# Attention scores on 62 and 64 array rows instead of 48 and 50, the added rows filled by zeros

## The reference

```python
h = layernorm(x) * (1 + ca) + sa
q, k, v = split(h @ w_in.T)                  # 16 heads, Hd = 16, N = 1024
scores = einsum('bhqd,bhkd->bhqk', q, k) * Hd ** -0.5
scores = where(causal, -inf, scores)
x = x + ga * ((softmax(scores) @ v) @ w_out.T + b_out)
h = layernorm(x) * (1 + cb) + sb
x_prev = shift_by_one_token(h)
xr = mu_r * h + (1 - mu_r) * x_prev;  xk = mu_k * h + (1 - mu_k) * x_prev
x = x + gb * sigmoid(xr @ W_r.T) * (square(relu(xk @ W_k.T)) @ W_v.T)
```

## Time and profile before

| what | value |
|---|---|
| median of 3 runs | 2016.91 us (1999.79 to 2022.92) |
| the profiled execution | 2004.49 us |
| its span, first to last instruction | 2002.6 us |
| around the span | 1.9 us |
| TensorE busy | 1685.5 us, 84% |
| VectorE, ScalarE, GpSimd busy | 1106.7, 917.5, 614.1 us |
| mean granted TensorE clock | 0.784 |

### The profile page before, as it was taken

One profiled execution on the slowest core, in us unless ns is written; L12 is line 12 of the kernel. 1 busy time (PEld: TensorE's weight loads), 2 busy tenths in 40 slices (PEclk: granted clock), 3 DMA queues, 4 the chain that ended last, 5 costly groups with the idle time before them and its releaser, 6 DMA issues.

```text
span 2002.6 us, 34555 instructions
## 1 busy us (share of the span) xinstructions
PE 1685.5 (84%) x10856; PEld 939.6 (47%) x10856; DVE 1106.7 (55%) x2246; ACT 917.5 (46%) x1859; POOL 614.1 (31%) x750
## 2 busy tenths in 40 slices
PE   4798898888888888889888898988888888889855
PEld 2443444444544445445444445444454444544444
DVE  4666546656465554655557454565546566555332
ACT  2055445455345543455445443545534545444522
POOL 2012112323333231343224333232333323233454
PEclk7596858678886987778796787768778687977865
DMA  2311131111221122111211113111122112211010
GB/s 89 78 39 39 47 84 47 33 44 47 80 59 36 46 57 72 42 46 44 84 44 48 33 49 87 47 33 46 44 81 61 33 38 61 65 40 49 28 48 16
DMA packets 79864, 103.37 MB, mean 52 GB/s; under 512 B 22576, under 2 KB 43320, under 8 KB 79680
## 3 DMA queue, kind: packets, MB, share of 16 engines
q1 hardware_dynamic: 76544, 91.86, 17.0%
q0 software_dynamic: 2560, 8.39, 1.1%
q10 hardware_dynamic: 576, 0.79, 0.2%
HBM read 31.74 MB, written 8.94 MB: 20 GB/s over the span
## 4 chain that ended last, share of the span: by engine, by line
PE 64%; DVE 14%; ACT 9%; issue 8%; POOL 2%; DMA 1%; SPq 1%; ACTq 0%; DVEq 0%; POOLq 0%
PE val_ps L1120 16%; PE col_ps L1051 13%; PE dense_ps L1130 9%; PE row_ps L1088 8%; DVE max_a L874 7%; PE dense_ps L1131 6%; PE dense_ps L1132 6%; PE row_ps L1099 4%; PE dense_ps L1149 3%; ACT weights L715 3%; ACT h_hi L758 1%; PE row_ps L1069 1%; DVE mix_out L990 1%; DVE stats_c L900 1%; ACT k_part L746 1%
## 5 line engine op out<-in xcount | busy, mean ns | idle before, releaser
L715 ACT ACTIVATE weights<-col_ps 128x512 f32<-128x512 f32 (+2 forms) x1280 | 631.7, 558 | 675.6 <-PE col_ps L1051 674.5
L874 DVE TENSOR_REDUCE max_a<-row_ps 128x1 f32<-128x512 f32 (+3 forms) x896 | 541.9, 644 | 357.4 <-PE row_ps L1099 255.9
L1088 PE MATMUL row_ps<-k_stack,q_stack 48*128 48x512 f32 (+3 forms) x1536 | 462.9, 458 | 83.8 <-DVE max_a L874 64.4
L1051 PE MATMUL col_ps<-q_stack,k_stack 50*128 50x512 f32 (+3 forms) x1536 | 460.1, 492 | 87.0 <-ACT weights L715 79.7
L604 POOL TENSOR_SCALAR_AFFINE_SELECT weights<-weights 128x512 f32<-128x512 f32 x256 | 164.4, 642 | 877.0 <-ACT weights L715 875.2
L1120 PE MATMUL val_ps<-weights,v_ones 128*32 128x512 f32 (+3 forms) x3072 | 417.3, 623 | 4.7 <-POOL weights L604 4.5
L1051 PEld LDWEIGHTS col_ps<-q_stack,k_stack 50*128 50x128 f32 x1536 | 208.3, 219 | 329.3 <-ACT weights L715 194.5
L1088 PEld LDWEIGHTS row_ps<-k_stack,q_stack 48*128 48x128 f32 x1536 | 242.1, 236 | 196.1 <-DVE max_a L874 142.0
L874 DVE TENSOR_REDUCE max_b<-row_ps 128x1 f32<-128x384 f32 (+3 forms) x384 | 214.3, 594 | 205.1 <-PE row_ps L1099 203.1
L1099 PE MATMUL row_ps<-mask_fill,mask_ident 64*128 64x64 bf16 (+1 forms) x2048 | 172.2, 240 | 0.0
L1099 PEld LDWEIGHTS row_ps<-mask_fill,mask_ident 64*128 64x128 bf16 x2048 | 88.0, 113 | 42.0 <-issue 32.5
(11 more groups left out here) (122 smaller groups left out, 2191.6 us busy)
## 6 DMA issues: line engine op xcount, KB each, us to landing
q_stack<-q_part SPq DMA_DIRECT2D x384, 64.0 KB, 2.2
k_stack<-k_part SPq DMA_DIRECT2D x372, 64.0 KB, 2.2
xa<-in_x SPq DMA_DIRECT2D x8, 1024.0 KB, 5.6
att<-val_out SPq DMA_DIRECT2D x64, 128.0 KB
recips<-recip_rows SPq DMA_DIRECT2D x32, 256.0 KB
xq<-in_x SPq DMA_DIRECT2D x28, 256.0 KB, 4.0
out<-xq POOLq DMA_DIRECT2D x28, 256.0 KB, 2.7
q_stack<-max_rows SPq DMA_DIRECT2D x256, 4.0 KB
```

The costliest lines, as they stand in the source:

```text
L715: nc.scalar.activation(weights[:, t % 2, heads[0]:heads[-1] + 1:2, 0:q1 - q0], col_ps[bank][:, 0:n * (q1 - q0)].rearrange("p (h q) -> p h ...
L874: nc.vector.reduce_max(dest, bank[:, 0:len(heads) * (k1 - k0)].rearrange("p (h k) -> p h k", h=len(heads)), AX_X).then_inc(max_done, 1)
L1051: last = nc.tensor.matmul(col_ps[bank][:, i * (q1 - q0):(i + 1) * (q1 - q0)], stack_at(k_stack[s % 2], rows, heads[i], P * j, P * (j + 1)) ...
L1088: last = nc.tensor.matmul(banks[odd][:, n * width:(n + 1) * width], stack_at(q_stack[stack], rows, heads[n], P * i, P * (i + 1)), stack_at ...
```

## The change

The two rows with the maximum move from 48 and 49 of each half to 62 and 63 (`MAX_AT`), in `place_max`. Column scores read all 64 rows of a half, row scores 62 rows. Rows 48 to 61 of both `q_stack` buffers are set to zero once, by two memsets on POOL in the setup; in `k_stack` those rows are ones as before, so the products there are zero. The same matmuls run in the same order, and each writes what it did.

```diff
@@ -44,6 +44,7 @@
 MROWS = 2
 ROW_TILE = 64
+MAX_AT = ROW_TILE - MROWS
@@ -463,7 +464,7 @@ place_max
-                        row, lo = ROW_TILE * odd + ROWS + part, 8 * (2 * part + odd)
+                        row, lo = ROW_TILE * odd + MAX_AT + part, 8 * (2 * part + odd)
@@ -569,8 +570,10 @@ setup of POOL
-            nc.gpsimd.memset(neg_half[:], -0.5).then_inc(consts_zero, 1)
-            pool.wait_ge(consts_zero, 1)
+            nc.gpsimd.memset(neg_half[:], -0.5)
+            for stack in q_stack:
+                nc.gpsimd.memset(stack[:].bitcast(F32), 0.0).then_inc(consts_zero, 1)
+            pool.wait_ge(consts_zero, 2)
@@ -1047,7 +1050,7 @@ score_columns
-                        rows = slice(ROW_TILE * odd, ROW_TILE * odd + ROWS + MROWS)
+                        rows = slice(ROW_TILE * odd, ROW_TILE * (odd + 1))
@@ -1083,7 +1086,7 @@ row_pair
-                        rows = slice(ROW_TILE * odd, ROW_TILE * odd + ROWS)
+                        rows = slice(ROW_TILE * odd, ROW_TILE * odd + MAX_AT)
```

## The result

| | before | after |
|---|---|---|
| median of 4 runs, us | 2015.77 (1999.79 to 2022.92) | 1951.78 (1943.63 to 1962.56) |
| ratio, 95% interval | | 0.9696 (0.9618 to 0.9774) |
| the profiled execution, us | 2004.49 | 1943.63 |
| its span, us | 2002.6 | 1941.7 |
| mean granted TensorE clock | 0.784 | 0.830 |

The kernel is 3.0% faster; 8.7% was forecast (1840 of 2016 us). The time lies in the stated range (1755 to 1975), but the size is a third of what was said. Rival 1 gave 1941 us at a clock near 0.83, and that is what the profiled execution shows.

The account below looks back on a forecast made before the run. TensorE, busy 84% of the span at a mean clock of 0.784, was taken as the bound. 2002.6 (span) - 165 (clock) + 0 (rows) + 0 (setup) = 1838, plus 1.9 around it: 1840 us, range 1755 to 1975.

Parts of the forecast that it names:

- Rival 1: Whole kernel: only one fill counts, or the effect is proportional to added rows; clock near 0.83, 1941 us; chance 0.20.
- That only the clock could carry a gain: TensorE's granted clock: the one large term, 165 us off the span, with all other terms zero.
- Setup and widening at zero: POOL's two memsets, 3.5 us, hidden under 21 us idle; wider score operands add no matmul time: both zero.
- rival 2: TensorE's clock: no effect, it ignores rows or zeros don't count; 2004 us within 1%; chance 0.13.
- The price of 1.45: Whole span: 1.45 us at half clock hold the work of 1 us at full clock, taken from repeated steps and quarters.
- 1735 / (1 - 0.31x) + 2: Whole kernel: time in us with share x at half clock; 1735 us is the span wholly at full clock.
- The upper bound of 47 ns for two rows more: Score matmuls: if the step from 48 to 50 rows were real, widening would cost at most 72 us; zero was taken.
- I take it that the fill lifts quarters 1 and 3 to what quarter 2 shows now, 0.88, and quarters 0 and 2 to the best that a quarter 0 shows now, 0.94: Clock in the four quarters of a batch: mean rises to 0.91, span falls to 1838 us, 165 us less.
- VectorE's maxima are late next: TensorE's waits for VectorE's maxima: next limit if TensorE gets faster; VectorE already busy 81% of a full-clock pair of steps.
- Rival 3: Whole kernel: nearly always full clock, quarters at 0.97, 1770 us; chance 0.08.
- Rival 4: Step 4 of quarter 3 and its like in quarters 0 and 1: gaps lower the clock, 2047 us; chance 0.07.

Follow-up runs that it names:

- e5: Changed kernel with both scores on 32 rows of a half, a third of the score products and the column scores' maximum left out: 2147.18 us, 1.073 of before.
- e1: Changed kernel with row scores back on 48 rows, column scores staying on 64: 1970.19 us, 0.990 of the kernel before.
- e3: Changed kernel with column scores back on 50 rows and taken without the maximum, row scores staying on 62: 1971.31 us, 0.989 of the kernel before.
- e2: Changed kernel with row scores on 64 rows too, so both kinds read 64: 1949.96 us, 0.982 of the kernel before.
- e6: Changed kernel with VectorE's maxima taken over the first half of each block's keys: 1848.45 us, 0.926 of the kernel before.
- e4: Changed kernel with both kinds of scores on 48 rows, column scores taken without the maximum: 2005.55 us, 1.004 of the kernel before.
- e8: Changed kernel with a 256-column product of zeros ahead of column-score pairs except in steps 1 and 5: 1936.97 us, 0.972 of the kernel before.
- e15: Changed kernel with row scores on 64 rows and two 512-column products of zeros ahead of each column-score pair in steps 0, 3, 4, 11: 1924.36 us.

## Why the prediction was partly right

- **That only the clock could carry a gain: right.** The score matmuls' own time is the same at the same clock (437 and 483 ns), and untouched groups got faster.
- **Setup and widening at zero: right**, 3.55 us under an idle time that still has 17.71 us.
- **Busy time alone does not set the clock (against rival 2): right.** 98% busy at half clock was the pointer; e5 is the proof in the other direction, with TensorE 87% busy at a clock of 0.706, where the kernel before has 84% at 0.784 and the changed one 83% at 0.830. The reading of the Trainium skill ("TensorE: Matmul & The Clock Gate", Part 1: The HAM clock gate) as busy time alone would have left 2004 us, and these runs do not agree with it.
- **The price of 1.45: right.** The formula 1735 / (1 - 0.31x) + 2 gives, with each profile's own clock, 1941 us for the changed kernel (1943.63 measured), 1960 for e1 (1967.26), 1971 for e3 (1966.19), 1937 for e2 (1943.15). It does not hold where the work changes: e6 lies 79 us under it, and e5, far outside the clocks it was taken from, 43 us over.
- **The upper bound of 47 ns for two rows more: a misreading that cost nothing.** It set column scores on 50 rows against row scores on 48; e4's column scores on 48 rows take 483 ns. That ScalarE's banks explain the difference was not tested.
- **"I take it that the fill lifts quarters 1 and 3 to what quarter 2 shows now, 0.88, and quarters 0 and 2 to the best that a quarter 0 shows now, 0.94": wrong.** This is the failed step, a term whose mechanism is right and whose size is not. It took 0.91 for a clock that measured 0.830, so 165 us where 61 came. Four things it left out. It read the clock of quarter 2 as a level that any richer work reaches, though quarter 2 adds whole products of 128 rows, far more than 14 rows of zeros. It laid 0.91 over the whole span, also over the first 92.3 and the last 107.6 us, which hold almost no scores and stood at 0.66 each before the change: by its own formula about 31 us of the 165, an estimate from these windows. It treated the falls as rare accidents that a little help avoids, from the one pair of quarters 3 in which batch 4 and batch 5 differ; but 45 of 57 falls sit in the same two steps of every quarter, and 40 of 60 do with the fill. And it ignored that the waits in the timeline, cited beside a fall, are untouched by the change. How much each of the four weighs was not measured, and why the rise stopped at 0.83 stays open.
- **"VectorE's maxima are late next": of no weight for the clock.** The idle time before the row scores rose from 83.8 to 95.0 us, and 67.5 of it is VectorE's, 3.1 us more than before. Taking half of the keys out of the maxima gave time and hardly any clock (e6).
- **Rival 1: right in time (1941), clock (0.83) and, as far as shown, its second mechanism**, the effect in proportion to the added rows: either fill alone gives about half. Its first, that the row scores' fill to 62 counts for nothing, has e2 (1950 us, no further gain at 64) and e3's clock (0.803 to 0.824) against it. It had a chance of 0.20. That it hit the time to 3 us of the profiled execution is partly luck: its mean came from thirds chosen by hand. Quarter 1 did come to its 0.77, but quarter 2 did not rise, and a quarter of the gain came in batch 0, which no part of the prediction looked at.
- **Rival 3: not seen.** No quarter has a mean of 0.97.
- **Rival 4: not seen.** Quarter 3 has a mean of 0.83 over batches 1 to 6, against 0.78 before, and no run with the fill was slower.

## What to carry to other kernels

Where TensorE is busy all the time and its granted clock still swings, look at what the matmuls occupy as well as at the gaps: here paired matmuls on a part of each half's rows could be padded with zero rows at no cost of their own (437 and 483 ns for 435 and 482), and 14 rows more in 28% of the matmuls gave 2 to 3%. Before forecasting how far a clock will rise, list the places where it falls, over all batches and not in one: this change left those places as they were and only shortened the stretches behind them. And lay a forecast clock only over the stretches that hold the changed work. Price half-clock time from the same steps of the program at both clocks (here 1.41 to 1.50, not 2); that number carried over to four kernels within 7 us.

## What the runs showed that I had not expected

- Rows of zeros count for the clock: the changed kernel and e2 gain through rows that hold nothing but zeros in `q_stack`, and even products of a wholly zero weight tile lifted the clock from 0.830 to 0.867 (e8).
- Taking work away can slow the kernel: with a third of the score products left out (e5, 32 rows), it took 7.3% longer, at a clock of 0.706.
- Adding work can make it faster: e15's 380 products of zeros, which kept TensorE busy for 141.5 us in its trace, left it 1.9% faster than the changed kernel.
- With the maxima over half of the keys the kernel gained about 5% at nearly the same clock, though the waits for VectorE named in the trace fell by only 36 us: another 22 us was hidden in TensorE's busy time, in pairs whose second matmul started late.
